# Gated scan and mixture of experts on one core: work inside a sequence in another order, scales in 8 operations

## What is computed

```python
xn = layernorm(x)
g, v, d = xn @ Wg + bg, xn @ Wv + bv, xn @ Wd + bd
y1 = linear_scan(sigmoid(g) * tanh(v), 0.001 + 0.998 * sigmoid(d))   # along each sequence
scores = sigmoid(xn @ Wg2.T + bg2 + bias)                            # 8 experts, the best 2 of each token
combined = sum over the 2 of score * (gelu(xn @ W1[e].T + b1[e]) @ W2[e].T + b2[e])
shared = gelu(xn @ Ws1.T + bs1) @ Ws2.T + bs2
out = x + y1 + shared + combined
```

## Time and profile before

| | us |
|---|---|
| median of three runs | 738.0 |
| the three runs | 737.7, 738.0, 742.22 |
| the profiled execution, its own time | 739.86 |
| the profiled execution, span of the trace | 737.6 |
| PE busy in the span | 666.5 |
| DVE busy | 525.4 |
| ACT busy | 432.3 |
| POOL busy | 305.1 |

### The profile page before, as it was taken

One profiled execution on the slowest core, in us unless ns is written; L12 is line 12 of the kernel. 1 busy time (PEld: TensorE's weight loads), 2 busy tenths in 40 slices (PEclk: granted clock), 3 DMA queues, 4 the chain that ended last, 5 costly groups with the idle time before them and its releaser, 6 DMA issues. The chain is left out here.

```text
span 737.6 us, 20181 instructions
## 1 busy us (share of the span) xinstructions
PE 666.5 (90%) x5816; PEld 517.8 (70%) x5817; DVE 525.4 (71%) x1381; ACT 432.3 (59%) x738; POOL 305.1 (41%) x261
## 2 busy tenths in 40 slices
PE   2689898999999998889999999999999999998784
PEld 1246555555656474568888888888889888887663
DVE  4579797988889898866666667666666676675542
ACT  6766858686777766435555555555555555554542
POOL 2015251524333343315455456446446545544321
PEclk9899999999999999999999999999999999999998
DMA  7307171716152624113233234233333334333231
GB/s 268 143 11 154 65 161 42 172 29 170 36 164 36 164 58 115 44 44 57 58 64 57 58 64 64 52 62 64 56 58 65 56 61 68 52 56 53 51 53 15
DMA packets 54170, 57.53 MB, mean 78 GB/s; under 512 B 13204, under 2 KB 48916, under 8 KB 54136
## 3 DMA queue, kind: packets, MB, share of 16 engines
q1 hardware_dynamic: 38456, 38.42, 20.4%
q0 software_dynamic: 15680, 18.69, 16.0%
HBM read 38.53 MB, written 18.55 MB: 77 GB/s over the span
## 5 line engine op out<-in xcount | busy, mean ns | idle before, releaser
L1098 PE MATMUL bank<-W,arena 128*128 (+1 forms) x2304 | 304.7, 274 | 20.4 <-DVE arena L821 17.4
L1090 PE MATMUL bank<-rows,W 128*128 128x256 f16 (+1 forms) x1920 | 301.8, 295 | 4.4 <-issue 3.3
L1098 PEld LDWEIGHTS bank<-W,arena 128*128 128x128 f16 x2304 | 221.4, 98 | 64.8 <-DVE arena L821 27.7
L1090 PEld LDWEIGHTS bank<-rows,W 128*128 (+1 forms) x1920 | 186.6, 99 | 59.4 <-issue 4.5
L464 POOL DMA_INDIRECT out<-arena,slot_add x71 | 120.5, 1697 | 180.6 <-ACT arena L647 170.9
L545 ACT ACTIVATE arena<-bank,par 128x256 f32<-128x256 f32 x256 | 134.3, 560 | 83.3 <-PE bank L1090 78.2
L820 DVE TENSOR_SCALAR arena<-arena,par 128x256 f16<-128x256 f32 x284 | 102.7, 362 | 78.7 <-ACT arena L545 49.3
L821 DVE SCALAR_TENSOR_TENSOR arena<-arena,par 128x256 f16<-128x256 f32 x284 | 138.7, 488 | 10.1
L419 POOL DMA_INDIRECT lists<-entry,place x64 | 80.7, 1261 | 119.5 <-DVE entry L817 102.4
L453 POOL DMA_INDIRECT rows<-xhl_rows,slot_list x71 | 77.7, 1094 | 52.9 <-DMA slot_list<-lists 26.9
L1078 PE MATMUL bank<-rows,W 128*128 128x512 f16 x288 | 67.5, 394 | 6.2 <-ACT arena L531 6.2
(11 more groups left out here) (152 smaller groups left out, 528.9 us busy)
## 6 DMA issues: line engine op xcount, KB each, us to landing
stage<-in_w SPq DMA_DIRECT2D x32, 512.0 KB, 7.0
b2row<-in_b SPq DMA_DIRECT2D x39, 128.0 KB
arena<-in_x SPq DMA_DIRECT2D x8, 512.0 KB
xhl_rows<-W SPq DMA_DIRECT2D x8, 512.0 KB
out<-arena SPq DMA_DIRECT2D x8, 512.0 KB
W<-in_w SPq DMA_DIRECT2D x4, 512.0 KB, 8.4
rows<-xhl_rows,slot_list POOLq DMA_INDIRECT x71
out<-arena,slot_add POOLq DMA_INDIRECT x71
```

Of the source, the lines that this page charges most:

```text
L1090: ins = T.matmul(bank_, weights(w, wp * HALF + c * H + j * P, P), rhs[:, 2 * xp + c, :], start=n == 0, stop=n == 3 * KD - 1)
L1098: ins = T.matmul(banks[t // 2][:, (t % 2) * D:(t % 2 + 1) * D], h[:, hp, t * P:(t + 1) * P], weights(w, (2 + wp) * HALF + j * D, D), start ...
```

## The change

1. `squares`: W1's two parts are taken after projections 1 and 4, W2's two parts after the first and second gelu (in the last sequence the second and third), where all but the first stood before the first gelu. `score` moves ahead of projection 5. Because of the later place, W1's squares of set 8 write their unused output over dead columns.
2. `norm_sum` stays after unit 0 of PE (unit 2 in the last sequence), writes to the bank of the ranks instead of the transposes' bank, and so waits for `places`. It is two matmuls of 2 columns instead of one of 4.
3. `scales` has 8 operations instead of 13: integer arithmetic on the exponent takes the place of the square root, the reciprocal and two multiplications.
4. On DVE `places` moves from behind split 2 to behind split 0 (in the last sequence ahead of `shared_result`), the residuals from behind splits 3 and 4 to behind 2 and 3, `low_part` (l = 0) from behind splits 5 and 7 to behind split 4 and behind `add_bias`. `scan_input` no longer waits for the decay's projection.
5. On PE both pairs of transposes move one unit up, and `ranks` moves ahead of the first `layer1`.
6. On POOL `fill_entries` of the next sequence moves ahead of the scatter.
7. In the last sequence the three parts of `tables` move from behind splits 0, 1, 2 to behind splits 1, 2, 4, the residuals and `scales` of set 8 come ahead of the last part, and `low_part` of set 8 follows splits 5, 6, 7 instead of standing mostly at the end. PE waits for the second layer's low parts only after the first three `layer1` of slot 0.

```diff
@@ scales, DVE @@
-                seq(V.tensor_reduce(total, sums[:, 0:4].rearrange("p (l q) -> p l q", l=2), AX.X, ALU.add))
-                seq(V.tensor_scalar(total, total, 1e-24, None, ALU.max))
-                seq(V.tensor_scalar(root.bitcast(I32), total.bitcast(I32), EXPONENT, None, ALU.bitwise_and))
-                seq(V.tensor_scalar(root.bitcast(I32), root.bitcast(I32), 0.5, float(127 << 22), ALU.mult, ALU.add))
-                seq(V.tensor_scalar(pw[:, 0:2].bitcast(I32), root.bitcast(I32), EXPONENT, None, ALU.bitwise_and))
...
-                seq(V.tensor_scalar(pw[:, 2:3].bitcast(I32), bound.bitcast(I32), EXPONENT, None, ALU.bitwise_and))
-                seq(V.reciprocal(ip, pw))
-                seq(V.tensor_scalar(inv, pw, 1.0 / TOP, None, ALU.mult))
-                own.mark(V.tensor_scalar(scl, ip, TOP, None, ALU.mult))
...
+                seq(V.tensor_scalar(total.bitcast(I32), sums.bitcast(I32), SMALLEST, 0.5, ALU.max, ALU.mult))
+                seq(V.tensor_scalar(root_i, total.bitcast(I32), EXPONENT, None, ALU.bitwise_and))
+                own.mark(V.tensor_scalar(scl_i[:, 0:2], root_i, -1.0, float((268 - 63) << 23), ALU.mult, ALU.add))
...
+                seq(V.tensor_scalar(bound, root[:, 0:1], 2.0 ** 68, b1red[:, bass.ds(n, 1)], ALU.mult, ALU.add))
+                own.mark(V.tensor_scalar(set_[:, 0:1], root[:, 0:1], 2.0 ** 63 / (TOP * XSCALE), None, ALU.mult))
+                seq(V.tensor_scalar(pw_i, bound.bitcast(I32), EXPONENT, None, ALU.bitwise_and))
+                own.mark(V.tensor_scalar(set_[:, 1:2].bitcast(I32), pw_i, -1.0, float(268 << 23), ALU.mult, ALU.add))
+                V.tensor_scalar(set_[:, 2:3], root[:, 1:2], 2.0 ** 63 / TOP ** 2, pw[:, 2:3], ALU.mult,
@@ scan_input, DVE @@
-                dve.wait_ge(ev_act, b * EVENTS + 3 * ch + 3 + RING)
+                dve.wait_ge(ev_act, b * EVENTS + 3 * ch + 2 + RING)
@@ sequence, DVE, inside the eight units @@
                     split_wide(b, i)
                     if i == 0:
+                        if not last_:
+                            places(b, u)
                         scan(b, 1)
...
+                    if i in (2, 3):
+                        residual(b, u, i - 2)
+                    if last_ and i in (1, 2, 4):
+                        tables((1, 2, 4).index(i))
+                    if i == 4 and not last_:
+                        low_part(b + 1, 0, 0)
+                    if last_ and i >= 5:
+                        low_part(b + 1, (i - 5) // 2, (i - 5) % 2)
...
                 else:
                     add_bias(b + 1, 1 - u)
+                    low_part(b + 1, 0, 1)
@@ norm_sum, PE @@
-                T.matmul(sums[:, 0:4], onesf[:, :], ssq, start=True, stop=True).then_inc(norm_ok, 1)
+                halves = ssq.rearrange("p (l q) -> p l q", q=2)
+                for part in range(2):
+                    ins = T.matmul(sums, onesf[:, :], halves[:, :, part], start=part == 0, stop=part == 1)
+                ins.then_inc(norm_ok, 1)
@@ sequence, PE @@
-                    if i == 0 and not last_:
-                        pe.wait_ge(xT_ok, b * 2 + 2)
-                        norm_sum(b + 1, ps_t)
+                    if i == (2 if last_ else 0):
+                        pe.wait_ge(place_ok, b + 1)
+                        norm_sum(b + 1, ps_l[:, 128:130])
+                    if i == 1:
+                        pe.wait_ge(scan_ok, b * 2 + 2)
+                        scan_transposes(b, 0)
@@ sequence, ACT @@
+                    if i == 1:
+                        squares(b + 1, 0, 0)
+                    if i == 4:
                         score(b)
+                        squares(b + 1, 0, 1)
...
                 for i in range(KH):
                     gelu_wide(b, u, i)
+                    if i in ((1, 2) if last_ else (0, 1)):
+                        squares(b + 1, 1, i - last_)
```

More of the change, by code:

```diff
@@ L52 @@
 EXPONENT = 0x7F800000
+SMALLEST = float(48 << 23)
 EPS = 1e-5
@@ L494, in squares @@
                 o = n * WSET + l * 2 * HALF + part * HALF // 2
+                if isinstance(n, int) and n == NW - 1:
+                    o = (at + 4 * SEQ if l == 0 else n * WSET) + part * HALF // 2
                 ins = A(W[:, bass.ds(o, HALF // 2)], landing(n, l)[:, part * HALF // 2:(part + 1) * HALF // 2],
@@ L854, in sequence @@
                     if i == 0:
+                        if not last_:
+                            places(b, u)
                         scan(b, 1)
-                    if i == 3 and not first:
-                        dve.wait_ge(o_out, b * 16)
-                    if i in (3, 4):
-                        residual(b, u, i - 3)
-                    if last_:
-                        if i < 3:
-                            tables(i)
-                        if i == 4:
-                            scales(NW - 1)
-                        if i >= 6:
-                            low_part(NW - 1, 0, i - 6)
-                        continue
-                    if i == 1:
+                    if i == 1 and not last_:
+                        scales(b + 1)
+                    if i == 3 and last_:
                         scales(b + 1)
                     if i == 2:
-                        places(b, u)
-                        x_low(b + 1)
-                    if i in (5, 7):
-                        low_part(b + 1, 0, (i - 5) // 2)
+                        if not last_:
+                            x_low(b + 1)
+                        if not first:
+                            dve.wait_ge(o_out, b * 16)
+                    if i in (2, 3):
[6 more added lines that the diff above has]
+                        low_part(b + 1, (i - 5) // 2, (i - 5) % 2)
                 if last_:
-                    for part in range(2):
-                        low_part(NW - 1, 1, part)
                     keep_entries(0, 0, first=True)
                     parameters(0, 0)
+                    low_part(b + 1, 1, 1)
                 else:
                     add_bias(b + 1, 1 - u)
+                    low_part(b + 1, 0, 1)
             def keep_entries(n, u, first=False):
@@ L1162, in sequence @@
                     make(b, u, k)
-                    if k == (2 if last_ else PROJ):
+                    if k == (2 if last_ else PROJ - 1):
                         ranks(b)
                     if k == 2 and first:
-                        norm_sum(0, ps_y[0])
+                        norm_sum(0, ps_y[0][:, 0:2])
                 for i in range(KH):
@@ L1196, in sequence @@
                         x_transposes(b + 1, 0)
-                    if i == 6 and not last_:
+                    if i == 5 and not last_:
                         pe.wait_ge(xT_ok, b * 2 + 3)
@@ L1200, in sequence @@
                 if last_:
-                    for l in range(2):
-                        for part in range(2):
-                            pe.wait_ge(stage_used[l][part], NW)
+                    for part in range(2):
+                        pe.wait_ge(stage_used[0][part], NW)
                     pe.wait_ge(rowsT_ok, 1)
@@ L1207, in sequence @@
                         first_layer(0, j, 0, w)
+                    for part in range(2):
+                        pe.wait_ge(stage_used[1][part], NW)
             pe.nop().then_inc(scanT_ps, 2)
@@ L1211, in _ @@
             pe.wait_ge(const_ok, 5)
-            norm_sum(-1, ps_y[0])
+            norm_sum(-1, ps_y[0][:, 0:2])
             pe.wait_ge(xhl_ok, 1)
```

67 lines of the change are left out of this document (18 added, 49 removed).

## The result

Beside the kernel before, on the chips of the first comparison, the changed kernel takes 743.4 us (median of 14 runs, 741.7 to 747.0) against 739.7 us (14 runs, 735.9 to 743.9). The ratio is 1.0046, 95% interval 1.0026 to 1.0067. The forecast was 725.7, and 731.0 the end of its range. The profiled execution took 746.44 us, its span is 744.6. Later runs of the same unaltered kernel on another chip gave 726.0 us, a ratio of 0.984. Both numbers belong to the result, and the difference goes with the chip.

What follows compares the result with a forecast made beforehand. The prediction took a ring through VectorE to set each sequence's period, with TensorE the next bound. 1.0 (start) + 12.7 (seven sequences) − 1.4 (last sequence) = 12.3 us off 738.0 gave 725.7 us, range 718.5 to 731.

Steps and rivals of the forecast that it cites:

- The step that failed: TensorE's order in each sequence: transposes moved one unit up were to wait for nothing; residual 0 ends about when needed.
- TensorE as the next bound: Splits 6 and 7 wait for second layers to free buffers; split 7 idles 0.77 us, period 33.51 instead of 32.74.
- the port: Scatters now beside split 1 share VectorE's ports with GpSimd: 0.1 us or less, left out.
- late weights: Rival: W1's second part lands too late; at 13 us the period is 36.7 and the time 745; chance 0.04.
- The seven sequences: First best-two search to last sequence's logits: 230.2 us against 242.85, 12.7 us saved.
- The squares: Squares on ScalarE moved behind the gelus: scan 0 to split 0 falls from 4.84 to 3.56 us, 1.28 per sequence.
- The scales: VectorE between splits 1 and 2: 8 operations instead of 13 take 1.47 us instead of 2.77, saving 1.3 per sequence.
- At the start: Shorter scales ahead of the first sequence, where nothing hides them: 1.0 us saved, once.
- The rival of 32.74: VectorE's ring alone sets the period, buffers don't bind: 32.74 us instead of 33.51, time 721.1; chance 0.15.
- The last sequence: Later slot tables delay the rows: slot 0 starts at 42.5 us instead of 41.14, a loss of 1.4.
- a whole scatter: Rival: a split waits for a whole scatter, 1.26 us more in each of six rings, time 733.3; chance 0.07.
- the ring: Chain through VectorE, with ScalarE between scan 0 and split 0, that sets the sequence period: 35.32 us before, 33.51 forecast.

Runs made afterwards that it cites:

- s1: Kernel before with only the new `scales` and `norm_sum`: 737.58 us against 739.97, ratio 0.9964.
- e5b: Changed kernel without the scatters (GpSimd only raises their semaphore), run again on a chip with late signals in the slots: 726.81 us, ratio 0.9825.
- e6b: Changed kernel with VectorE's loop written out and the last sequence's slot tables back behind splits 0, 1, 2, on a late-kind chip: 721.95 us, ratio 0.9744.
- e7_both: Changed kernel with loop written out, tables early, and scatters of all sequences but the last held until both residuals are done: 728.74 us, ratio 0.9825.
- a2_after_third: Changed kernel, unaltered, run beside edited ones on a chip where nothing jams: 726.0 us against 737.56, ratio 0.984.
- b1_before_again: Kernel before, unaltered, run again for its trace beside the changed kernel's second run: 736.5 us.
- e5: Changed kernel without the scatters (GpSimd only raises their semaphore), on a chip where nothing jams: 726.72 us, ratio 0.9843.
- groups one and three: Runs on two chips without the jam: loop written out, scatters late or store late in the changed kernel; kernel before 736.89 and 737.56 us.
- group four: Changed kernel without scatters, with loop written out, with scatters late, or with loop written out and tables early: 726.72, 723.32, 729.51, 720.43 us.
- three edits: To the changed kernel, singly: VectorE's loop written out, 723.65 us; scatters after both residuals, 726.9; store of split rows after both residuals, 726.96.

## Why the prediction was wrong, and where it was right

**The step that failed** is in the part on TensorE as the next bound: "The transposes moved up find their scans and residuals done". It looked at the transposes' inputs. Of the other side, the residual that waits for the transposes, it took for granted that TensorE's signal comes with the end of the row. On the chips of the first comparison it comes 4.7 us later. In the order before, the second residual stood a unit later and waited 0.5 us at most; in the new order it meets the jam. The change moves the scatters forward as well, and the prediction priced them for the port alone. Four sequences are 37.67 to 38.41 us long, instead of 33.7 on a chip without the jam, together 17.8 us more. The median missed the forecast by 743.4 − 725.7 = 17.7, about as much. (Between the spans of the two traces, 744.6 and 724.5, lie 20.1 us; the other 2.3 are in the slots.)

What makes the signals late is shown only in part. The scatters must be there: s1 and e5b, on one chip, say so. VectorE's loop has a part in the 4 us wait, but not in the lateness as such. The gap came in all eight looped sequences of the two traces and in no written-out one, those of e6b on a chip of the late kind included. But raises are late in written-out sequences too, 3.68 us in s1, 3.38 us in e7_both, and 0.95 us behind the second transposes of sequence 0 of the changed kernel. The kernel before has late raises as well, behind the transposes of x, by 1.3 to 1.4 us in sequences 1 to 4.

An open rival to the loop's waits is plain timing. The second transposes end 3.50 us after the first scatter's start in the kernel before, 6.80 us after it in the looped sequences of the changed kernel, and 6.58 us in the written-out ones of e6b, whose scatters also go out over 11.0 us instead of 9.3. The changed kernel with and without its loop wasn't run on one chip of the late kind, no run changes the loop and keeps this timing, and none moves the residual without the scatters. Why the raises come late was not found.

The slower rival of the prediction, late weights, forecast 745 and so came close to the number, but had no part: from 40 to 280 us in the trace of the first comparison no wait of a computing engine ends with a transfer.

**The rest of the sum** can be checked in the trace of a2_after_third, where the signals come on time. Its stretches, cut as above:

```profile
32.64:262.49 229.85, 220.93 (x1670) 139.71 (x1669) 200.66 (x480) 171.61 (x255) 83.35 (x84) 0.99 0.37 101
262.49:305.36 42.87, 35.54 (x240) 21.01 (x238) 34.37 (x92) 21.18 (x31) 13.67 (x12) 0.92 0.23 69
```

And one steady sequence on VectorE, with the search at its start (L769), scan 0 (first L748), split 0, places (L794), scan 1, split 1, the scales (L689 to L702), split 2, x_low (L730), the residuals with split 3 between them, and splits 6 and 7:

```profile
166.38 0.24 DVE L769 SCALAR_TENSOR_TENSOR rt<-bank,small 128x32 f32<-128x32 f32 x1
...
172.25 1.22 DVE L748 TENSOR_TENSOR_SCAN arena<-arena 128x512 f32<-128x512 f32 x1
...
175.89 0.49 DVE L805 TENSOR_SCALAR arena<-arena,PT 128x512 f16<-128x512 f32 x1 [1.83 <-ACT arena L541]
...
177.08 0.18 DVE L794 TENSOR_TENSOR rt<-bank,small 128x32 f32<-128x32 f32 x1
...
178.19 1.23 DVE L748 TENSOR_TENSOR_SCAN arena<-arena 128x512 f32<-128x512 f32 x1
179.33 0.46 DVE L805 TENSOR_SCALAR arena<-arena,PT 128x512 f16<-128x512 f32 x1
...
180.49 0.15 DVE L689 TENSOR_SCALAR small<-bank 128x2 int32<-128x2 int32 x1
...
182.09 0.49 DVE L805 TENSOR_SCALAR arena<-arena,PT 128x512 f16<-128x512 f32 x1
...
184.42 0.68 DVE L754 SCALAR_TENSOR_TENSOR arena<-bank,arena 128x512 f32<-128x512 f32 x1
185.02 0.66 DVE L805 TENSOR_SCALAR arena<-arena,PT 128x512 f16<-128x512 f32 x1
185.71 0.77 DVE L806 SCALAR_TENSOR_TENSOR arena<-arena,PT 128x512 f16<-128x512 f32 x1
186.40 0.68 DVE L754 SCALAR_TENSOR_TENSOR arena<-bank,arena 128x512 f32<-128x512 f32 x1
...
191.06 0.49 DVE L805 TENSOR_SCALAR arena<-arena,PT 128x512 f16<-128x512 f32 x1 [0.42 <-PE bank L1086]
...
192.82 0.48 DVE L805 TENSOR_SCALAR arena<-arena,PT 128x512 f16<-128x512 f32 x1 [0.48 <-PE bank L1086]
```

- *The seven sequences:* forecast 230.2 us, measured 229.85.
- *The squares:* scan 0 to split 0 forecast 3.56 us, measured 175.89 − 172.25 = 3.64, against 4.84 in the earlier trace rows.
- *The scales:* forecast 1.47 us, measured 182.09 − 179.33 less the split's 1.19 = 1.57; s1 puts the saving at 1.18 where I had taken 1.3. At the start, from the first of these operations to the low part behind them, it is 26.72 − 24.17 = 2.55 us, against 3.65 in both traces of the kernel before: 1.1 us saved, forecast 1.0. The search itself comes no earlier than in b1_before_again (32.64 and 32.65).
- *TensorE as the next bound:* splits 6 and 7 wait for second layers, 0.42 and 0.48 us, where 0.8 was forecast ahead of split 7 alone. From split 1 to split 7 it is 192.82 − 179.33 = 13.49 us, forecast 1.33 + 12.0. The period is 33.62 to 33.74 us in the loop and 33.2 outside it. That the six average 33.51, the forecast to the hundredth, is luck: the forecast was read from a looped sequence and made no difference between the two. The rival of 32.74 falls here. Periods of 32.71 to 32.76 came only on chips with late signals, in single sequences, and why isn't known.
- *The last sequence:* forecast 42.5 us to slot 0, measured 42.87. In the trace of the first comparison, route_ok, forecast 29.9 us after the logits, came at 310.38 − 280.05 = 30.33, and TensorE waited for the rows:

```profile
319.58 1.01 PE L1130 MATMUL bank<-ident,rows 128*128 128x128 f16 x8 [3.96 <-DMA rows<-xhl_rows,slot_list]
```

- *The port:* no split waited for a whole scatter; beside scatters a split's first operation takes 0.66 us instead of 0.49. The Trainium skill, "SBUF — State Buffer", section "Who interferes with whom", says that whoever issues first holds the shared pair of ports for its whole instruction. The rows show something like it on GpSimd's side alone: in sequence 1 of the changed kernel a scatter that begins inside x_low takes 1.61 us, where most take 0.96. That fits a scatter that waits for the rest of x_low. GpSimd is not in the ring, so it costs nothing on such a chip, as e5 shows.

```profile
82.19 1.22 DVE L730 TENSOR_TENSOR W<-W 128x1024 f16<-128x1024 f32 x1
```

```profile
82.62 1.61 POOL L420 DMA_INDIRECT lists<-entry,place x1 [0.31 <-issue]
```

So on a chip where the signals come on time the sum held, 726.0 for 725.7; against the kernel before on that chip (737.56) the saving is 11.6 us, forecast 12.3. It lacked a case for signals that come late. The table of times before held a hint of it that I had read past: of three runs two took 738 us and one 742.2, and the kernel before shows the same two heaps, some 4.5 us apart, in the comparisons on other chips of the late kind. On the chips of groups one and three, where the records are complete, it took 736.4 to 738.8 only. The hint is weak: on the chip of group four, also complete, it took 736.1 to 741.1.

## What to carry to other kernels

Before moving the wait of one engine closer to the work of another, ask how much time the signal in between has, and don't take the modelled end of a matmul for the moment of its signal. A wait that the trace puts down to "remote" means that the signal came at a time when nothing ended; compare the raise of the semaphore with the row. Where a result differs between chips, run the unaltered kernel beside every edit on one chip: here three edits seemed to cure what the chip had cured. Write a short loop out if an engine in the ring runs it: it gave 1.6 us here, and 0.45 us in each looped sequence by the traces. On a chip with late signals the version with it, and with the tables early, took 722 us, where the changed kernel took 743 and 748 in the comparisons on other such chips.

## What the runs showed of the hardware

- On some chips TensorE's semaphore raises come up to 4.9 us behind the row's end in sequences with scatters, and then in a burst (161.72, 161.80, 161.92, 162.00). On others every recorded one comes 0.01 us behind the row's end.
- On one chip of the late kind the kernel without the scatters had no late raise in its sequences (e5b), and one with them had raises up to 3.68 us late (s1). The store of split rows was in both.
- Late raises came in looped and in written-out sequences. The wait of 4 us at the second residual came in looped ones alone, in all 8 of two traces.
- VectorE's loop cost 0.45 us (changed kernel) to 0.8 us (kernel before) per sequence on chips without the jam.
- A pause of 2.8 us of TensorE was followed by a granted clock of 0.54, and a second layer took 2.31 us instead of 1.47.
